# Layer 0 of a four-layer graph network on one Trainium2 core: six row tiles turned on the chip instead of read twice

## The reference

```python
A = adj + jnp.eye(N)
D = 1.0 / jnp.sqrt(jnp.sum(A, axis=1))
A = A * D[:, None] * D[None, :]
out = A @ (x @ W0)
x = layernorm(x + relu(out + b0))
```

## Time and profile before

| | us |
|---|---|
| median of 3 runs (lowest, highest) | 1433.82 (1432.99, 1435.67) |
| the profiled execution, its own time | 1435.09 |
| its span, first to last instruction | 1433.5 |
| TensorE busy | 1322.4 (92%) |
| VectorE busy | 906.7 (63%) |
| ScalarE busy | 546.0 (38%) |

### The profile page before, as it was taken

One profiled execution on the slowest core, in us unless ns is written; L12 is line 12 of the kernel. 1 busy time (PEld: TensorE's weight loads), 2 busy tenths in 40 slices (PEclk: granted clock), 3 DMA queues, 4 the chain that ended last, 5 costly groups with the idle time before them and its releaser, 6 DMA issues.

```text
span 1433.5 us, 11332 instructions
## 1 busy us (share of the span) xinstructions
PE 1322.4 (92%) x4138; PEld 658.3 (46%) x4138; DVE 906.7 (63%) x1194; ACT 546.0 (38%) x473; POOL 189.3 (13%) x211
## 2 busy tenths in 40 slices
PE   3888886899998999999999999999999999999993
PEld 1333333444454444446445455544445444544451
DVE  4777777888866000003126362799978987898576
ACT  4434344877640000000211011455564656455333
POOL 0000002000010000001000000133421352124111
PEclk9999999899999999999999999999999999999997
DMA  9999992000025776757667249698876888688301
GB/s 380 426 418 418 418 415 94 25 0 0 0 81 162 193 195 193 194 162 242 216 215 222 76 136 334 231 369 320 304 284 243 335 309 303 238 304 322 138 0 50
DMA packets 78000, 321.26 MB, mean 224 GB/s; under 512 B 8684, under 2 KB 20587, under 8 KB 61035
## 3 DMA queue, kind: packets, MB, share of 16 engines
q1 hardware_dynamic: 77931, 320.40, 62.9%
HBM read 316.94 MB, written 3.43 MB: 223 GB/s over the span
## 4 chain that ended last, share of the span: by engine, by line
PE 83%; DMA 9%; DVE 5%; ACT 1%; issue 1%; SPq 0%; POOL 0%; ACTq 0%; DVEq 0%; POOLq 0%
PE ps L1351 30%; PE ps L1152 10%; PE ps L1189 10%; PE ps L1086 10%; DMA ring<-in_adjR 8%; PE ps L1011 6%; PE ps L1146 5%; PE ps L1261 2%; PE ps L1372 1%; PE ps L1333 1%; PE ps L1170 1%; PE ps L1373 1%; PE ps L1126 1%; DMA y<-in_adj 1%; PE ps L1171 1%; PE ps L1220 1%
## 5 line engine op out<-in xcount | busy, mean ns | idle before, releaser
L1351 PE MATMUL ps<-arena,x 128*128 128x512 f32 (+1 forms) x1092 | 438.9, 562 | 2.9 <-ACT shared L914 1.6
L1351 PEld LDWEIGHTS ps<-arena,x 128*128 128x128 f32 x1092 | 206.1, 190 | 231.4 <-issue 225.2
L907 ACT ACTIVATE arena<-arena,bench 128x3328 f32<-128x3328 bf16 x78 | 239.7, 3075 | 188.3 <-PE ps L1351 176.0
L1011 PE MATMUL ps<-ring,bench 128*128 128x512 f32 (+1 forms) x364 | 171.8, 617 | 51.0 <-DMA ring<-in_adjR 49.1
L2023 DVE TENSOR_TENSOR arena<-arena,ring 128x3328 f32<-128x3328 f32 x51 | 184.6, 3620 | 27.2 <-ACT arena L907 26.6
L1152 PE MATMUL ps<-ring,x 128*128 128x512 f32 (+1 forms) x364 | 176.1, 565 | 0.0
L1189 PE MATMUL ps<-ring,x 128*128 128x512 f32 (+1 forms) x364 | 149.2, 563 | 0.0
L1011 PEld LDWEIGHTS ps<-ring,bench 128*128 128x128 f32 x364 | 71.2, 207 | 130.3 <-issue 99.1
L1723 DVE SCALAR_TENSOR_TENSOR bench<-b,cols,ps 128x128 f32<-128x128 f32 x26 | 7.3, 342 | 182.3 <-PE ps L1126 182.3
L664 POOL TENSOR_TENSOR ring<-ring,nid 128x128 f32<-128x128 f32 x51 | 87.7, 1720 | 208.9 <-DMA ring<-in_adjR 208.9
L1146 PE MATMUL ps<-arena,shared 128*128 128x512 fp8e4 (+1 forms) x364 | 103.6, 366 | 6.4 <-DVE shared L1528 6.4
(11 more groups left out here) (296 smaller groups left out, 1361.9 us busy)
## 6 DMA issues: line engine op xcount, KB each, us to landing
ring<-in_adjR SPq DMA_DIRECT2D x77, 1664.0 KB, 8.9
ring<-in_adjB SPq DMA_DIRECT2D x312, 256.0 KB, 3.1
arena<-in_adjR SPq DMA_DIRECT2D x27, 1664.0 KB, 8.5
shared<-in_adj SPq DMA_DIRECT2D x7, 1664.0 KB, 12.7
es<-in_adj SPq DMA_DIRECT2D x7, 1664.0 KB, 13.4
xT<-in_adj SPq DMA_DIRECT2D x6, 1664.0 KB, 12.8
y<-in_adj SPq DMA_DIRECT2D x6, 1664.0 KB, 13.6
ring<-in_adjB SPq DMA_DIRECT2D x52, 128.0 KB, 2.3
```

Of the source, the lines that this page charges most:

```text
L907: A_(E[n % 3], below[n % 3], ACT.Exp, bias=tt_[:, t * HEADS + k:t * HEADS + k + 1], scale=-WIN).then_inc(e_exp, 1)
L1011: op = mm(ps[:, b, 0:w], lhsT=scaled[:, t % 4], rhs=turned_tile[t % 2][:, o_:o_ + w], start=(t == 0), stop=(t == TILES - 1))
L1351: last = mm(ps[:, b, 0:w], lhsT=x[:, t], rhs=E[n % 3][:, o_:o_ + w], start=(t == 0), stop=(t == TILES - 1))
```

## The change

The tiles are taken from the last to the first: step s works on tile 25 - s, and row tile n read is tile 25 - n.

- The first six row tiles read (tiles 25 to 20) are also turned by TensorE: 26 transposes of 128x128 each into PSUM, in seven cuts of up to four, which ScalarE (three cuts) and VectorE (four cuts) copy out to strips in `arena` and `gru`. So `strip(t)` holds, for the turned tile t, the 768 columns of these six row tiles.
- A turned tile is read without those columns: 2560 of 3328, 1280 KB. Blocks 5 and 6 of the product and 768 columns of the pattern come from the strip. Blocks 5 and 6 go first.
- SyncE reads four row tiles, `x`, a turned tile, two more row tiles, a turned tile, and then row tiles as far as four ahead of the last scanned one. A row tile of the first six is overwritten only when it is turned.
- The least element is no longer a TENSOR_REDUCE. A TENSOR_SCALAR clamps to +-3e38 with `accum_out`, and writes its 128x3328 output to a place that is free.
- VectorE takes the six first scans, then the strips, and `scale` (reciprocal and scaling) is a function of its own. The other 20 scans are spread over 24 steps. `pattern(s)` waits until TensorE is through with step s - 1, since its output covers the strip of that step.
- The last turned tile comes in two transfers (1536 and 1024 columns). TensorE puts the first six W0 products behind blocks 1 to 6 of it. The flag is made at its beginning. `finish0` has moved to `summed0`, a space of its own, and the weights of later layers wait for the last group of `y`.

```diff
+TURNED = 6
+PLAIN = TILES - TURNED
+SC = TURNED * P
+MC = NP - SC
+HALF = 3 * MAX_WIDTH
...
+        CUTS = [list(range(t, min(t + 4, TILES))) for t in range(1, TILES, 4)]
+        CUTS[-1].append(0)
+        CUT_ACT, CUT_VE = (0, 2, 4), (1, 3, 5, 6)
+        def scanned_until(s):
+            return min(TILES, TURNED + max(0, (s + 1) * PLAIN // NAT_STEPS))
...
+            for n in range(4):
+                nat_load(n)
             sp.dma_start(x[:], d["x"]).then_inc(x_in, 16)
+            tile_load(0)
+            nat_load(4)
+            nat_load(5)
+            tile_load(1)
+            loaded = TURNED
+            for s in range(TILES):
+                if s >= 2:
+                    sp.wait_ge(tile_used, s - 1)
+                    sp.wait_ge(pos_done, s - 1)
+                    tile_load(s)
+                while loaded < min(TILES, scanned_until(s - 2) + 4):
+                    nat_load(loaded)
+                    loaded += 1
...
+            def strip_copies(n):
+                for q in CUT_ACT:
+                    act.wait_ge(rows_turned, n * len(CUTS) + q + 1)
+                    for dst, src in strip_parts(n, q):
+                        op = A_(dst, src, ACT.Copy)
+                    op.then_inc(strip_act, 1)
+            for n in range(TILES):
+                row_sums(n)
+                if 1 <= n <= TURNED:
+                    strip_copies(n - 1)
...
+            def turn_rows(n):
+                pe.wait_ge(summed, n + 1)
+                for q, tiles in enumerate(CUTS):
+                    c = n * len(CUTS) + q
+                    if c >= 8:
+                        cut_copied(pe, c - 8)
+                    for k, t in enumerate(tiles):
+                        last = nc.tensor.transpose(ps[:, cut_bank(n, q), k * P:(k + 1) * P], nat[n % 4][:, t * P:(t + 1) * P], ident[:])
+                    last.then_inc(rows_turned, 1)
...
+                for b in (0, 1, 2, 3, 4, 5, 6) if final else (5, 6, 0, 1, 2, 3, 4):
...
+                    if b == 0:
+                        pe.wait_ge(tile_in[s % 2], (s // 2 + 1) * 16)
...
+                    moving = strip(t)[:, o_ - MC:o_ - MC + w] if o_ >= MC else turned_tile[s % 2][:, o_:o_ + w]
...
+                    if final and b:
+                        if b == 1:
+                            pe.wait_ge(flag_ready, 1)
+                        product(0, b - 1, (b - 1) % 2, W0[:], Z0)
...
-                v.tensor_reduce(mn[:, t:t + 1], nat[t % 4], AX.X, ALU.min)
+                v.tensor_scalar(kept, nat[n % 4], -BIG, BIG, ALU.max, ALU.min, accum_out=mn[:, t:t + 1],
+                                saturate=False).then_inc(nat_used, 1)
...
+                ge(ve, tile_used, s)
...
+                v.tensor_scalar(pos8[:, t, MC:], strip(t), 0.0, None, ALU.is_gt, saturate=False)
```

More of the change, by code:

```diff
@@ L19 @@
 CW = 2 * GW
+TURNED = 6
+PLAIN = TILES - TURNED
+SC = TURNED * P
+MC = NP - SC
+PITCH = NP // 4
+NAT_STEPS = 24
+BIG = 3e38
 HEADS = 3
@@ L396, in NU @@
             return ps[:, 5 + par, 0:GW]
[L398 to L404, removed]
         def is_(g, k):
@@ L999, in _ @@
+            for n in range(TURNED):
+                turn_rows(n)
+            pe.wait_ge(strip_act, TURNED * len(CUT_ACT))
+            pe.wait_ge(strip_ve, TURNED * len(CUT_VE))
+            for s in range(TILES):
+                t = TILES - 1 - s
+                first, final = s == 0, s == TILES - 1
+                if s == WEIGHTS_PE:
                     weight_products()
-                if t == WEIGHTS_VE + 3:
+                if s == WEIGHTS_VE + 3:
                     spread_w2()
-                pe.wait_ge(xs_done, t + 1)
@@ L1010, in _ @@
+                    if not first and t // BT == b:
                         itself()
-                    op = mm(ps[:, b, 0:w], lhsT=scaled[:, t % 4], rhs=turned_tile[t % 2][:, o_:o_ + w], start=(t == 0),
-                            stop=(t == TILES - 1))
-                    if t == TILES - 1:
+                    moving = strip(t)[:, o_ - MC:o_ - MC + w] if o_ >= MC else turned_tile[s % 2][:, o_:o_ + w]
+                    op = mm(ps[:, b, 0:w], lhsT=scaled[:, s % 4], rhs=moving, start=first, stop=final)
@@ L1022, in _ @@
-            pe.wait_ge(flag_ready, 1)
-            groups(pe, lambda g, par, n: product(0, g, par, W0[:], Z0))
+                    if final and b:
+                        if b == 1:
+                            pe.wait_ge(flag_ready, 1)
+                        product(0, b - 1, (b - 1) % 2, W0[:], Z0)
+            for g in range(NB - 1, GROUPS):
+                product(0, g, g % 2, W0[:], Z0)
             def spread_f1(b):
@@ L1470, in pattern @@
[L1470 to L1479, removed]
+                ve.wait_ge(D_done, s + 1)
+                if s >= 4:
+                    ve.wait_ge(tile_used, s - 3)
@@ new lines, in strip_copies, with pattern @@
+            def strip_copies(n):
+                for q in CUT_VE:
+                    ve.wait_ge(rows_turned, n * len(CUTS) + q + 1)
+                    for dst, src in strip_parts(n, q):
+                        op = v.tensor_copy(dst, src)
+                    op.then_inc(strip_ve, 1)
+            def pattern(s):
+                t = TILES - 1 - s
+                ge(ve, tile_used, s)
+                if s == TILES - 1:
+                    ve.wait_ge(flag_row, 1)
+                    step(v.tensor_reduce(row[0:1, 0:1], ps[0:1, 7, 2 * P:3 * P], AX.X, ALU.min))
+                    v.tensor_scalar(flag[0:1, 0:1], row[0:1, 0:1], 0.0, None, ALU.is_ge).then_inc(flag_ready, 1)
+                if s == 0:
+                    ve.wait_ge(strip_act, TURNED * len(CUT_ACT))
+                    ve.wait_ge(strip_ve, TURNED * len(CUT_VE))
+                v.tensor_scalar(pos8[:, t, MC:], strip(t), 0.0, None, ALU.is_gt, saturate=False)
+                ve.wait_ge(tile_in[s % 2], (s // 2 + 1) * 16)
+                cut = HALF if s == TILES - 1 else MC
+                op = v.tensor_scalar(pos8[:, t, 0:cut], turned_tile[s % 2][:, 0:cut], 0.0, None, ALU.is_gt, saturate=False)
+                if cut < MC:
+                    ve.wait_ge(last_half, 16)
+                    op = v.tensor_scalar(pos8[:, t, cut:MC], turned_tile[s % 2][:, cut:MC], 0.0, None, ALU.is_gt, saturate=False)
+                op.then_inc(pos_done, 1)
@@ new lines, in _ @@
+            for n in range(TURNED):
+                scan(n)
+                if n:
+                    strip_copies(n - 1)
+            strip_copies(TURNED - 1)
+            ve.wait_ge(x_in, 16)
+            for s in range(4):
+                scale(s)
+            for s in range(TILES):
+                if 4 <= s + 1 < TILES:
+                    scale(s + 1)
+                for n in range(scanned_until(s - 1), scanned_until(s)):
+                    scan(n)
+                pattern(s)
+                if s == WEIGHTS_VE:
```

118 lines of the change are left out of this document (69 added, 49 removed).

## The result

The changed kernel takes **1427.09 us** (median of 8 runs, 1425.83 to 1430.99) against 1433.70 (8 runs, 1432.12 to 1436.25): ratio 0.9950, 95% interval 0.9940 to 0.9961, a gain of about 7 us. The forecast was 15.2 us, 1418.6. The time lies in the range, and the gain is less than half of the forecast. The profiled execution took 1426.91 us, its span is 1425.2; that of before took 1435.09, so between the two profiles it is 8.2 us.

A forecast was written before the change was run, and what follows sets the result against it. Layer 0's first stage was taken as bound by transfers. The last tile's start gains 13.8 us, the end 3.4, the clock costs 2: gain 15.2 us, median 1433.82 to 1418.6 us, range 1410 to 1429.

The forecast's parts named there:

- What bounds the stage: Layer 0's first stage is bound by what it reads; one 1664 KB load takes 4.08 us, TensorE's tile 5.81 us.
- the shorter rows: Turned tiles of 1280 KB load in 3.14 us instead of 4.08; rival that they save nothing: 1440 us, chance 0.03.
- The clamp: VectorE's clamp with accumulated output over a row tile was taken at 1.95 us, its other end being 3.61 us.
- ScalarE's path: Sums and strip copies on ScalarE, taken to set the first product's start at 48.0 us.
- The first tile: TensorE's first product tile was to cost 2.6 us extra for the clock after idle time, bounds 0 and 2.6.
- The steps: Tile steps before the last tile: ten stall at 7.22 us, 15 take 5.81; last tile starts at 210.0 us.
- The clock in the steps: Falls of TensorE's clock in the tile steps were to cost 2 us, ends 0 and 8.5.
- The end: From the last tile's start to the stage's end: 19.3 us instead of 22.7, a gain of 3.4 us.
- Behind layer 0: Everything after the stage waits on its end, so a shift of that end was taken as the whole kernel's.
- the slow clamp: Rival: VectorE's clamp runs at the reduction's pace, 5.0 us more, 1423.6 us; chance 0.26.
- Loads hidden wholly: Rival: the transfers never pause in the steps, last tile starts at 202.3 us, 1409 us; chance 0.12.
- that rival: TensorE's clock falls in every step, each tile 7.5 us, 1445 us; decides from a 7.06 us mean step; chance 0.08.

The follow-up runs named there:

- e11: e7 with the row tiles over the first 20 steps, so that no pause stands among them; 1424.8 us, ratio 0.9933.
- e1: Changed kernel with the clamp's accumulated output left out, the flag made from the diagonal alone; 1426.8 us, ratio 0.9945.
- e3: Changed kernel with the W0 products behind all blocks of the last tile again; 1430.6 us, ratio 0.9972.
- e7: e6 with the five early weight loads issued in step 0 as in e2; 1418.3 us, ratio 0.9886.
- e9: e6 with both parts issued at the end of the tile, leaving only the finer wait; 1422.9 us, ratio 0.9920.
- e2: Changed kernel with the five early weight loads issued in step 0 instead of steps 2 and 3; 1426.0 us, ratio 0.9938.
- e4: e2 with a row tile asked for one step earlier; 1425.6 us, ratio 0.9933.
- e6: Changed kernel with each turned tile read and awaited in two parts, the first issued after three of the old tile's five blocks; 1419.4 us, ratio 0.9896.
- e10: e6 with TensorE waiting for both parts, leaving only the earlier issue; 1421.0 us, ratio 0.9912.
- e5: The kernel before, unchanged, run once more for its trace alone; its span is 1433.4 us.
- e8: e7 with the row tiles spread over 25 steps and not 24; 1416.9 us, ratio 0.9873.

## Why the prediction was right in its direction and too high in its size

- **What bounds the stage, the shorter rows, the turned strips**: right. Steps take 5.81 us where no tile is late; twelve of the fourteen stalled ones take 7.05 us in the mean (6.3 to 7.5), and e11's in a row 7.13 to 7.18, for a forecast of 7.22.
- **The clamp**: the wrong end was taken. It is 3.62 us, not 1.95, as the rival said. The Trainium skill (VectorE: DVE Perf Modes, The perf-mode tier table) gives float32 `tensor_scalar` in SBUF twice the pace of `tensor_reduce`. The trace of e1 agrees for the clamp without an accumulated output, 1894 ns against 3612. With one it is 3620 ns, which only the run tells. The rival's price of 5.0 us was too high: the copies of one tile take about 2.2 us instead of 2.8 (in the chain four take 1.99 us), so a tile takes VectorE 40.41 - 34.16 = 6.25 us and not 7.0. The start is 49.15 instead of 48.0 us, and e1, without that delay, is no faster by more than its uncertainty. ScalarE's path was done at 47.55, as forecast.
- **The first tile**: 7.57 us, and 6.03 the second: +2.0 us together instead of +2.6, at a granted clock of 0.79. (By the rows the 2.6 should have been 8.53 - 5.81 = 2.7.) In e1, e3, e7 and e9 the first took 5.9 us, in the others 7.6 to 7.8, behind 1.2 to 2.1 us of idle time in both, so the size is luck in part. The Trainium skill (TensorE: Matmul & The Clock Gate, Part 4: PE-mode transpose) says that transposes do not count as busy for the clock in the same way. The trace disagrees for these of float32, which it lists as MATMUL: with only transposes run so far, the granted clock stands at 1.00 from 26 to 30 us, 26 of them taking 3.06 us (0.12 us each).
- **The steps**: this is the step that failed. "So 2 us of lag are free, ... about two free ones follow the beginning and each pause, and ten stall." Fourteen stalled, with 21.6 us instead of 14.1. The row tiles come in groups of 5, 5, 5 and 1; of these 5, 4, 4 and 1 stalled, so not two in each group were free but none or one. (By its own sentence the count would have been nine, since the last group has only one.) The lag that is free was too large: a tile that "alone needs some 5 us" takes 5.6 to 5.9 from issue to landing, which leaves 7.1 - 5.7 = 1.4 us, as much as the forecast gave a single row tile. And one row tile adds more at first: in e2, with nothing else in the queue, the first turned tile behind one takes 7.9 us, 2.2 more than the one ahead of it, and step 4 stalls at 6.73 us; why it is 2.2 and not 1.4 isn't settled. A pause can't give back 2.7 us either: a tile doesn't take less than alone, so at most the 1.4 come back.
  Twelve of the fourteen cost 14.9 us, 1.25 each, near their price. The other two are step 4, 2.75 us, and step 12, 3.9 us. So of the 7.5 us beyond the forecast, the higher count makes 3.4 (fourteen at 1.25 against ten at 1.41) and the two dear steps the other 4.1. Step 4 is late also by weight loads that I had not counted on this queue (without them, in e2, it is 1.8 us shorter). In step 12 the clock fell; it did so in e1 and e4 as well, at 9.9 and 10.1 us, and in the other profiles step 12 takes 6.9 to 7.8 us.
  That the time between a tile's issue and its use is what binds, e6, e9 and e10 show: with more of it the excess is 14.4 us, the last tile starts at 210.8 us, and the time is 1419.4. That these are nearly the forecast's own numbers for the kernel without that mending is chance.
- **The clock in the steps**: one fall to the lower level, in step 12, where TensorE waited 1.95 us and the granted clock went to 0.79 and 0.50. Six matmuls behind it took 4.32 us, where six behind another wait, at 118.65 us, took 2.84: about 1.5 us against the 2 counted.
- **The end**: 237.45 - 218.05 = 19.4 us (forecast 19.3), and e3 gives 3.5 us for the part (forecast 3.4; uncertainty 2). Right.
- **Behind layer 0**: "everything behind waits on that in turn" lost 0.9 us of 9.05: the shift had grown to 9.7 us at 844 us of the kernel before (in layer 3), and was 8.1 behind the wait that is shown at e5.

Together: 15.2 forecast; the last tile's start, clock included, 223.8 - 218.05 = 5.75 instead of 11.8 (start 1.15 worse, first two tiles 0.6 better, steps with the clock 5.5 worse); the end 0.1 less; 0.9 lost behind. That is the 8.2 us between the profiles; the medians are 6.6 us apart.

The rivals: the slow clamp was there and decided nothing. Loads hidden wholly: no, and not in e8 either. The clock fell once and not in every step; the mean step was (218.05 - 49.15) / 25 = 6.76 us, under the 7.06 from which that rival decided. The shorter rows did save.

## What to carry to other kernels

When loads get shorter and the queue was the bound, ask next what keeps it fed: with two buffers the time from a buffer's release to the next first use is what a load may take, and a larger transfer just ahead of it in the same queue counts against it: in e2 the first such load took 2.2 us longer, of 7.1 that it had. Releasing and awaiting a buffer in parts costs a semaphore and brought here as much again as the whole change. Where the mean need of two resources is nearly equal (5.75 and 5.81 us a step), it also matters how evenly the loads are spread: row tiles in 20 steps without a pause (e11) took 6.5 us more than in 24 with pauses (e7).

## What the runs showed of the hardware that was not expected

- Transposes alone bring the granted clock to 1.00 (26 to 30 us, 0.12 us each), after 0.51 in the six us before (0.22 us each). They don't keep it there: around a wait of 3.2 us it is 0.84 from 30 to 34 us and 0.73 from 34 to 38.
- A float32 clamp of 128x3328 takes 1894 ns, with an accumulated minimum 3620 ns, and is then listed as another instruction.
- Whether a wait lowers the clock isn't told by its length: 2.49 us at 78 us left it at 1.00, 1.95 us at 134 us brought 0.50.
- Behind 1.2 to 2.1 us of idle time, the first product tile ran in 5.9 us in four profiles and in 7.6 to 7.8 us in the others; what decides is open.
